# Cross attention: the row maxima in equal key ranges, one PSUM bank reduced by VectorE, the other copied to SBUF by ScalarE and reduced there

## The reference

```
scores = einsum('bhsr,bhlr->bhsl', q_r, k_r)     # 16 heads x 100 rows = 1600 query rows, 1444 keys, 64 features
attn   = softmax(scores, axis=-1)
ctx_c  = einsum('bhsl,bld->bhsd', attn, kv_r)
```

## Time and profile before

| | |
|---|---|
| median of 3 runs | 2658.78 us (2658.76 to 2662.6) |
| the profiled execution | 2658.4 us |
| its span, first to last instruction | 2656.6 us |
| cross attention, first to last maximum | 787.5 to 2409 us |
| one item of the cross attention, slot to slot | 50.74 us |
| mean granted TensorE clock | 0.965 of full speed |

### The profile page before, as it was taken

One profiled execution on the slowest core, in us unless ns is written; L12 is line 12 of the kernel. 1 busy time (PEld: TensorE's weight loads), 2 busy tenths in 40 slices (PEclk: granted clock), 3 DMA queues, 4 the chain that ended last, 5 costly groups with the idle time before them and its releaser, 6 DMA issues. The chain is left out here.

```text
span 2656.6 us, 46267 instructions
## 1 busy us (share of the span) xinstructions
PE 2418.3 (91%) x15794; PEld 1485.9 (56%) x15794; DVE 1582.5 (60%) x2401; ACT 1036.0 (39%) x1605; POOL 1839.9 (69%) x827
## 2 busy tenths in 40 slices
PE   7989849999966999999999999999999999999398
PEld 4455447777743555555555555555555555555288
DVE  6888848888744555555555555555555555551375
ACT  3233212222212444444444444444444444444143
POOL 2435427989852887887887887888788788789111
PEclk9999979999986999999999999999999999999699
DMA  4000026666663234224323323422422432320111
GB/s 127 14 25 19 13 78 180 178 185 177 179 158 65 61 69 89 64 55 90 70 61 82 77 62 69 91 62 67 90 64 55 90 69 61 85 49 17 39 44 37
DMA packets 310370, 210.36 MB, mean 79 GB/s; under 512 B 200055, under 2 KB 289355, under 8 KB 310177
## 3 DMA queue, kind: packets, MB, share of 16 engines
q1 hardware_dynamic: 310304, 209.51, 32.7%
HBM read 149.98 MB, written 59.48 MB: 79 GB/s over the span
## 5 line engine op out<-in xcount | busy, mean ns | idle before, releaser
L1663 POOL TENSOR_TENSOR x_acc<-x_acc,x_prob 120x1600 f32<-120x1600 f32 (+1 forms) x320 | 1150.0, 3594 | 76.0 <-ACT x_prob L1684 56.0
L1777 DVE TENSOR_REDUCE x_mx<-x_ring 115x2 f32<-115x1024 f32 (+4 forms) x672 | 781.1, 1162 | 528.7 <-PE x_ring L1909 528.7
L1684 ACT ACTIVATE x_prob<-x_scores 120x800 f32<-120x800 f32 (+1 forms) x768 | 601.6, 835 | 528.3 <-PE x_scores L1841 506.7
L1861 PE MATMUL x_context<-x_prob,x_kv 120*64 120x400 f32 (+1 forms) x3072 | 600.4, 512 | 0.0
L1909 PE MATMUL x_ring<-x_kh,x_qm 64*115 64x512 f32 (+4 forms) x1344 | 318.4, 470 | 58.6 <-DVE x_mx L1777 23.9
L1861 PEld LDWEIGHTS x_context<-x_prob,x_kv 120*64 120x64 f32 (+1 forms) x3072 | 186.2, 136 | 245.9 <-issue 168.6
L1909 PEld LDWEIGHTS x_ring<-x_kh,x_qm 64*115 64x115 f32 (+1 forms) x1344 | 119.7, 174 | 348.6 <-DVE x_mx L1777 326.8
L1663 POOL TENSOR_TENSOR x_acc<-x_prob 121x1600 f32<-121x1600 f32 x32 | 115.3, 3604 | 233.8 <-ACT x_prob L1684 233.8
L1841 PE MATMUL x_scores<-x_qh,x_dh 64*120 64x400 f32 (+1 forms) x1536 | 275.3, 354 | 0.0
L1841 PE MATMUL x_scores<-x_ql,x_dh 64*120 64x400 f32 (+1 forms) x1536 | 265.6, 341 | 0.0
L1841 PE MATMUL x_scores<-x_qh,x_dl 64*120 64x400 f32 (+1 forms) x1536 | 264.7, 340 | 0.0
(11 more groups left out here) (172 smaller groups left out, 3297.2 us busy)
## 6 DMA issues: line engine op xcount, KB each, us to landing
x_kr<-scratch_kr SPq DMA_DIRECT2D x64, 363.0 KB
x_kd<-scratch_kd SPq DMA_DIRECT2D x64, 332.8 KB
x_rden<-scratch_rden SPq DMA_DIRECT2D x68, 200.0 KB, 3.4
scratch_qh<-q_qsh SPq DMA_DIRECT2D x64, 200.0 KB, 3.8
scratch_ql<-q_qsl SPq DMA_DIRECT2D x64, 200.0 KB, 3.7
x_qm<-scratch_qh SPq DMA_DIRECT2D x64, 200.0 KB, 4.5
x_qh<-scratch_qh SPq DMA_DIRECT2D x64, 200.0 KB, 3.4
x_ql<-scratch_ql SPq DMA_DIRECT2D x64, 200.0 KB, 3.8
```

Source lines behind the costliest of these rows:

```text
L1663: pool.tensor_tensor(acc[0:rows, parity], first, prob[0:rows, c % PR], ALU.add).then_inc(acc_done.sem, 1)
L1684: act.activation(prob[0:rows, c % PR, u * HALF:(u + 1) * HALF].rearrange("p (j s) -> p j s", j=2), psc[0:rows, u, :, 0:BANK], ACT.Exp).the ...
L1777: dve.tensor_reduce(best[0:block_rows(r), :, r, i], ring[0:block_rows(r), :, 0:b - a], AX.X, ALU.max).then_inc(read_sem(u), 1)
L1861: mm = pe.matmul(pav[DC * s:DC * s + DC, j, 0:BANK], kv[0:rows, parity, c], prob[0:rows, c % PR, cols], start=c == 0, stop=c == LC - 1)
```

## The change

All units of the maxima use the key ranges 0-482, 482-964, 964-1444. Each pair is now two units, `("half", r, i, 0)` and `("half", r, i, 1)`, each with one bank of `ring`; banks alternate over all units. The t = 0 half is reduced by VectorE out of PSUM, and its bank is given back by that. The t = 1 half is copied by ScalarE into one of three SBUF buffers `half`, which gives its bank back, and is reduced by VectorE out of SBUF. ScalarE makes the copy of the pair behind the scores between its two exponentials, and that of a pair ahead of the scores before them. Steps keep the same number of pairs, the pairs keep their places, and the amount of matmul columns stays (1444 keys for each block and half).

```diff
--- before.py
+++ after.py
@@ -1401,6 +1401,7 @@
         ql = sb("ql", [P, 2, HALF], F32R)
         mx = sb("mx", [MR, 2 * MB, 3])
         negm = sb("negm", [MR, 2 * MB])
+        half = sb("half", [MR, 3, BANK + MR])
         mrow = sb("mrow", [2 * MB, MR], F32R)
         mq = sb("mq", [P, 2, MB * MR], F32R)
         prob = sb("prob", [LP, PR, QROWS])
@@ -1418,22 +1419,27 @@
         ring = ps("ring", [P, 2, 512])
 
 
-        wide = iter([("max", r, 0) for r in range(0, MB, 2)] + [("max", r, 2) for r in range(MB)])
-        narrow = iter([("max", r, 1) for r in range(MB)] + [("max", r, 0) for r in range(1, MB, 2)])
+        spans_left = iter([(r, i) for i in range(3) for r in range(MB)])
+
+        def largest():
+            r, i = next(spans_left)
+            return [("half", r, i, 0), ("half", r, i, 1)]
 
         order = []
         for c in range(LC):
             own = [("out",), ("dT", 0), ("kT", 2)] if c == 0 else []
             if c not in (0, 3, 5):
-                own.append(next(narrow))
-            own += [("scores", 0), ("scores", 1), next(wide) if c < LC - 1 else next(narrow), ("context",)]
+                own += largest()
+            own += [("scores", 0), ("scores", 1), *largest(), ("context",)]
             own += {2: [("dT", 1), ("dT", 2)], 4: [("den", 0), ("den", 1)],
                     LC - 1: [("mT",), ("kT", 0), ("kT", 1)]}.get(c, [])
             order.append(own)
-        assert next(wide, None) is None and next(narrow, None) is None
+        assert next(spans_left, None) is None
         beside = [[u for u in own if u[0] not in ("scores", "context")] for own in order]
         units = [u for own in beside for u in own]
-        first_max, *_, last_max = [u for u in units if u[0] == "max"]
+        first_max, *_, last_max = [u for u in units if u[0] == "half"]
+        copied = [u for u in units if u[0] == "half" and u[3] == 1]
+        trailing = [own[own.index(("scores", 1)) + 2] for own in order]
         last_steps = [u for u in units if u[0] == "dT"][-2:]
 
 
@@ -1476,6 +1482,7 @@
 
         dh_copied = sig("step_high_copied", 3, 3)
         max_ready = sig("maxima_ready", 1, 1)
+        half_read = sig("copied_half_read", len(copied), len(copied))
         den_stored = sig("denominators_stored", 16, 16)
         den_loaded = sig("denominators_loaded", 16, 16)
         den_inverted = sig("denominators_inverted", 1, 1)
@@ -1494,8 +1501,7 @@
 
 
         def keys_of(r, i):
-            ends = (0, 512 if r % 2 == 0 else (L - 512) // 2, L - 512, L)
-            return ends[i], ends[i + 1]
+            return 482 * i, min(482 * (i + 1), L)
         block = ctx.enter_context(nc.Block())
         N_MEMSET = 8
 
@@ -1671,7 +1677,7 @@
         @block.scalar
         def _(act):
             act.sem_inc(exp_done.sem, exp_done.credit)
-            for i in range(3):
+            for i in range(2):
                 act.sem_inc(rg.read[i], rg.credit("read", i))
 
             def exponentials(n, c, u):
@@ -1697,6 +1703,15 @@
                 wait_filled(act, n, u)
                 a, b = span[i]
                 act.copy(dh[:, parity, a:b], ring[:, rg.banks[u][0], 0:b - a]).then_inc(dh_copied.sem, 1)
+
+            def copy_half(n, u):
+
+                k = copied.index(u)
+                wait(act, half_read.sem, half_read.at(n, k - 2))
+                wait_filled(act, n, u)
+                a, b = keys_of(*u[1:3])
+                rows = slice(0, block_rows(u[1]))
+                act.copy(half[rows, k % 3, 0:b - a], ring[rows, rg.banks[u][0], 0:b - a]).then_inc(read_sem(u), 1)
 
             def save_den(n, j):
 
@@ -1725,11 +1740,16 @@
                             save_den(n, u[1])
 
                 for c in range(LC):
+                    for u in beside[c]:
+                        if u in copied and u not in trailing and made_at(n, u):
+                            copy_half(n, u)
                     if c == 0:
                         singles(beside[c])
-                    if not is_at(n, -1):
-                        for u in range(2):
+                    for u in range(2):
+                        if not is_at(n, -1):
                             exponentials(n, c, u)
+                        if u == 0 and made_at(n, trailing[c]):
+                            copy_half(n, trailing[c])
                     if c > 0:
                         singles(beside[c])
                     elif not is_at(n, -1) and not is_at(n, 0):
@@ -1770,12 +1790,18 @@
 
             best = mx[:].rearrange("p (t r) i -> p t r i", t=2)
 
-            def maximum(n, r, i):
-                u = ("max", r, i)
-                wait_filled(dve, n, u)
+            def half_maximum(n, u):
+                r, i, t = u[1:]
                 a, b = keys_of(r, i)
-                dve.tensor_reduce(best[0:block_rows(r), :, r, i], ring[0:block_rows(r), :, 0:b - a], AX.X,
-                                  ALU.max).then_inc(read_sem(u), 1)
+                to = mx[0:block_rows(r), MB * t + r, i:i + 1]
+                if t == 0:
+                    wait_filled(dve, n, u)
+                    dve.tensor_reduce(to, ring[0:block_rows(r), rg.banks[u][0], 0:b - a], AX.X,
+                                      ALU.max).then_inc(read_sem(u), 1)
+                else:
+                    wait_read(dve, n, u)
+                    dve.tensor_reduce(to, half[0:block_rows(r), copied.index(u) % 3, 0:b - a], AX.X,
+                                      ALU.max).then_inc(half_read.sem, 1)
 
             def turn_maxima(n):
                 u = ("mT",)
@@ -1791,10 +1817,10 @@
                             output(n, parity)
                         elif u[0] == "dT":
                             low_steps(n, 1 - parity, u[1])
-                        elif u[0] == "max":
-                            maximum(n, u[1], u[2])
+                        elif u[0] == "half":
+                            half_maximum(n, u)
                         elif u[0] == "mT":
-                            wait_read(dve, n, last_max)
+                            wait(dve, half_read.sem, half_read.at(n, len(copied)))
                             dve.tensor_reduce(negm[:], mx[:], AX.X, ALU.max, negate=True).then_inc(max_ready.sem, 1)
                             turn_maxima(n)
                     if c == 6:
@@ -1899,16 +1925,15 @@
                             wait(pe, ctx_normed.sem, ctx_normed.at(n - 1, h // 4 + 1))
                         mm = pe.matmul(ring[0:S, bank, 0:E], ctxn[:, h // 4, (h % 4) * S:(h % 4 + 1) * S],
                                        wco[:, h], start=h == 0, stop=h == H // 2 - 1)
-                elif u[0] == "max":
-                    r, i = u[1:]
+                elif u[0] == "half":
+                    r, i, t = u[1:]
                     if u == first_max:
                         pe.wait_ge(qm_loaded.sems[1 - parity], qm_loaded.done(n + 1, 1 - parity))
                     a, b = keys_of(r, i)
-                    for t in range(2):
-                        part = slice(DC * t, DC * t + DC)
-                        mm = pe.matmul(ring[0:block_rows(r), t, 0:b - a],
-                                       qm[part, 1 - parity, r * MR:r * MR + block_rows(r)], kh[part, a:b],
-                                       start=True, stop=True)
+                    part = slice(DC * t, DC * t + DC)
+                    mm = pe.matmul(ring[0:block_rows(r), bank, 0:b - a],
+                                   qm[part, 1 - parity, r * MR:r * MR + block_rows(r)], kh[part, a:b],
+                                   start=True, stop=True)
                 else:
                     pe.wait_ge(max_ready.sem, max_ready.at(n, 1))
                     mm = pe.transpose(ring[0:2 * MB, bank, 0:MR], negm[:], ident[0:MR, 0:MR])
```

## The result

The changed kernel takes 2560.31 us (median of four runs, 2558.02 to 2560.57) against 2659.51 for the kernel before in the same runs: a ratio of 0.9623, 95% interval 0.9606 to 0.964. It is 99 us faster, where 83 were forecast. Its profiled execution took 2560.12 us, with a span of 2558.3, 98.3 less than before. The time went where it was looked for: from the first pair of maxima to the first turned maxima (L1783, L1809 now) it is 11.2 us less (836.3 - 787.5 before, 825.6 - 788.0 after, starts of VectorE's first reduction and of its copy to `mrow`), and the 31 slots from there to the last turned maxima take 1486.4 us for 1573.5, 87.1 less. These two make up the whole 98.3; the rest of the kernel takes as long as before.

The account below looks back on a forecast made before the run. TensorE bounds the kernel, delayed by VectorE's hold on both banks. Gains of 2.36 us an item (73 over 31) plus 10 in the first pass took 2658.4 to 2575 us; good for 2560 to 2595, range 2547 to 2622.

Parts of the forecast that it names:

- first pass: 21 units with nothing beside them, at VectorE's pace; a pair was to need 1.53 us, gaining 10 us altogether.
- step 2: Second pair waits for VectorE's hold on both banks; first pair to context 2.12 us, without the wait 1.72: gain 0.40.
- step 1: Copy comes behind `save_context` on ScalarE and frees its bank late; context starts later: -0.14 us an item.
- Steps 6 to 10: Five steady steps of an item with no wait left: 16.05 us (5 x 3.21) in place of 17.78, gain 1.73.
- step 11: Last step of an item: pair to context 1.72 us in place of 2.10, gain 0.38.
- step 4: Same shape as step 1, first pair to context 1.99 us; gain 0.27 us an item.
- rival A: ScalarE frees banks late, so TensorE waits for it; 2617 us if half the gain in steps is lost; chance 0.16.
- The turn: End of an item: `negm` needs the last reduction; L1914 comes 1.81 us behind context in place of 1.53: -0.28.
- Rival C: VectorE's SBUF reductions block GpSimd, whose additions grow by about 0.5 us each; slower, 2820 us; chance 0.05.
- GpSimd's room: Before `out` wants the normalisation's first half, GpSimd has 1.4 us to spare an item, so the gain isn't cut.
- Rival D: TensorE's 0.40 us turns up as longer rounds elsewhere; only the first pass gains; 2649 us at best; chance 0.05.
- Rival B: Step 1 and the turn avoid their losses, a wait for dl shrinks; 3.2 us an item, 2549 us; chance 0.08.

Follow-up runs that it names:

- the held-up run: Changed kernel with a GpSimd memset of 3200 columns (2.8 us) ahead of each normalisation; 2624.35 us (one execution).
- the wrong order: Changed kernel with the copy of the pair behind the scores after both exponentials in place of between them; 2582.64 us, ratio 0.9722.

## Why the prediction was right, and where its terms were off

The rival theories of the experiments are out: equal ranges cost 20 us, splitting without the copy costs 17 (29 in the slots), copies behind the scores alone cost 18 (24 in the slots). The bank freed by ScalarE ahead of the scores is the cause of the 87 us in the slots. The 11 us of the first pass need only banks released apart. Not tried were copies with the unequal ranges of before, so what the ranges are worth beside the copies is open.

*The wait.* The 0.40 us of step 2 and 0.29 of step 1 were read from starts of matmuls against a step without a wait, not from the 189 us of the table of waits; 189 us in 1000 are 9.6 an item, and only a third of that (3.2, with the denominators below) delayed a start. Steps 6 to 10 gained 1.70 us (17.78 to 16.08) for 1.73, step 11 0.37 for 0.38, step 2 0.40, step 4 0.27 (1613.84 to 1615.56): these held to 0.03.

*Step 1* was the term with the wrong sign: +0.07 where -0.14 stood. I let each instruction occupy ScalarE for its whole duration. `save_context` is 0.83 us long, but the copy behind it started 0.72 after it (1602.96 to 1603.68); the copy is 0.57 long, and the exponential followed after 0.46 (1604.14). The hand-over was shorter than my 0.13, too. So the second pair's bank was late by some 0.13 us (the pair lasts 0.60, its second half by itself 0.47) and not by 0.32, and only that half waited while the first ran: context came 0.22 late and not 0.43. By the same 0.1 for each instruction, ScalarE's margin in a full step was larger than the 0.2 to 0.4 that I gave (it idles 0.6 us ahead of each first copy), so rival A didn't come. The double copy shows that it was the right thing to fear.

*The turn.* Context of step 11 to L1939 became 1.67 us, a loss of 0.14 for the 0.28 expected; but L1939 to `out` became 1.59 for 1.44, which I had not priced. The sum, -0.29, was right by luck: two errors cancelled. In the kernel with the last pair as one unit L1939 to `out` is 1.47.

*Not counted at all*: the denominators in step 4. They stood behind a pair held by VectorE too; context to L1920 and L1920 to the next scores are 1.39 and 1.45 us for 1.47 and 1.50, 0.13 an item. With 0.07 + 1.70 + 0.37 + 0.40 + 0.27 - 0.29 + 0.13 = 2.65 us the item of 48.06 us shown here is accounted for (50.74 - 48.06 = 2.68). The mean slot is 47.95, a gain of 2.8 for the forecast 2.36, 14 us in 31 slots. That is nearly the whole difference between 2575 and 2560. The 0.15 between 2.65 and 2.8 is spread: over 29 items the turn loses 0.24 in the mean, steps 6 to 10 gain 1.75, and steps 0, 3 and 5 gain 0.04 together. So the forecast held in its mechanism and in its large terms, and the time, 2560.31 us, lies within its range, at the near edge of the 2560 to 2595 that it called good. What it had too small were step 1 (by 0.2, with the wrong sign) and the denominators, put at nothing (0.13).

*First pass*: pairs are 1.49 us apart (818.98 to 820.47) for the 1.53 worked out, and it gained 11.2 us for 10. The granted clock is 0.50 in this stretch before and 0.55 after, so its rows say nothing of the slots.

*Rival C*, GpSimd blocked by VectorE's reads of SBUF, is out: the additions are 3.608 us for 3.592 in the same stretch. That is 0.4% longer, and it shows only in kernels with the copies (3.601 to 3.610 us in nine profiles, 3.592 to 3.595 in the three of kernels without). The sentence of the Trainium skill that was cited (SBUF — State Buffer, Who interferes with whom) holds by these numbers as far as blocking goes. Whether the 16 ns are the reads of VectorE or ScalarE's writes no run separates; the run with each copy made twice speaks against the number of writes, since it has 42 of them in a slot of 51.4 us and its additions are shorter (3.601 us) than the changed kernel's. *GpSimd's room* before the output matmuls is 1.5 us where 1.4 was forecast, by the held-up run: 2.8 us more cost 1.3 an item. *Rival D* is out with the result. *Rival B*'s 2549 was nearer to the time than what it rests on: only step 1 lost its loss, the turn kept it, and step 3's wait for dl stayed (1.97 us for 1.98).

## What to carry to other kernels

Where an engine waits for a buffer, subtract a stretch without the wait from one with it, start to start, and ask which of the waits is not covered by work in flight: here nine of 21, each removed by a copy of the pair ahead of it, and copies of the other 12 pairs gained nothing in the slots. A copy to a second engine pays even when it shortens nothing, if it lets two banks come free at once in place of one after the other; splitting the release without a second engine doesn't (29 us more in the slots). Count on an engine the distance between starts of back-to-back instructions (0.46 us here), not their duration (0.56), and price what a delayed exponential or copy does at the turn to the next item, for that is where the wrong order cost its 24 us.

## What the hardware showed that I had not expected

A gap of 1.5 us in TensorE's work can cost more than itself. In the kernel with GpSimd held up, ten slots in 30 were 1.65 us longer than the others. In each of the ten the granted clock fell right behind the gap, and the 16 output matmuls took 5.36 to 5.38 us for 3.70; in the one shown it was 0.60 over 4 us. In the other twenty the clock stayed at 1.00. The length of the gap doesn't tell the two kinds apart (1.54 to 1.75 us in the ten, 1.47 to 1.60 in the twenty), nor does what TensorE did before it in the two turns shown, 1.3 us of transposes in both. In the changed kernel, where TensorE idles 0.3 us there, the clock stays at full speed from 836 to 2310 us.
